# Second attention: the two normalisations of a step move from VectorE to ScalarE, with a bias made on GpSimd

## The reference, cut to what matters

```python
x = x + tanh(g_xattn[0]) * L0_xattn(layernorm(x), ctx, ctx)
x = x + tanh(g_ffn[0])   * L0_ffn(layernorm(x), ...)        # 64 experts, 8 per token, and a shared one
x = x + tanh(g_xattn[1]) * L1_xattn(layernorm(x), ctx, ctx, Wc, bc)
x = x + tanh(g_ffn[1])   * L1_ffn(layernorm(x), w_fc, w_proj)   # both products in emulated FP8

def L1_xattn(q, k, v, Wc, bc):      # 16 query heads of 16, 4 groups share a key and a value head
    scores = einsum('bghsd,bgtd->bghst', qh, kh) / sqrt(16)
    out = einsum('bghst,bgtd->bghsd', softmax(scores), vh)
    return out.reshape(b, s, 256) @ Wc.T + bc
```

## Time and profile before

| | |
|---|---|
| median of 3 runs | 1281.42 us (1279.56 to 1288.4) |
| the profiled execution's own time | 1274.8 us |
| its span | 1273.0 us |
| DVE busy over the span | 1050.5 us (83%) |
| PE / POOL / ACT busy | 883.2 / 718.4 / 702.0 us |
| second attention, steps 4 to 35 | from 883.4 to 1099.7 us of the span |

### The profile page before, as it was taken

One profiled execution on the slowest core, in us unless ns is written; L12 is line 12 of the kernel. 1 busy time (PEld: TensorE's weight loads), 2 busy tenths in 40 slices (PEclk: granted clock), 3 DMA queues, 4 the chain that ended last, 5 costly groups with the idle time before them and its releaser, 6 DMA issues.

```text
span 1273.0 us, 31296 instructions
## 1 busy us (share of the span) xinstructions
PE 883.2 (69%) x9384; PEld 626.0 (49%) x9394; DVE 1050.5 (83%) x2644; ACT 702.0 (55%) x1370; POOL 718.4 (56%) x800
## 2 busy tenths in 40 slices
PE   5789984465405888786777777756687778576665
PEld 3445552333204777675666666634455555322332
DVE  6789997988804889997589999966998888598998
ACT  4679994455303656655455555533555555515763
POOL 3557773777777565555347776456878882280000
PEclk9899995555557999999799999968899999888887
DMA  5977771222226999997899999985223330000011
GB/s 132 260 234 230 225 220 63 88 96 101 103 98 220 330 308 326 325 323 251 255 311 326 324 308 326 293 201 105 72 83 93 93 87 13 1 0 1 34 46 53
DMA packets 198114, 221.48 MB, mean 174 GB/s; under 512 B 44957, under 2 KB 176862, under 8 KB 197726
## 3 DMA queue, kind: packets, MB, share of 16 engines
q1 hardware_dynamic: 173406, 152.70, 39.0%
q0 software_dynamic: 24576, 67.14, 16.5%
HBM read 114.64 MB, written 105.12 MB: 173 GB/s over the span
## 4 chain that ended last, share of the span: by engine, by line
DMA 26%; DVE 23%; POOL 19%; issue 15%; PE 7%; ACT 5%; SPq 4%; DVEq 0%; POOLq 0%; ACTq 0%
DMA xs<-V 12%; POOL xs L757 7%; DMA V<-ys,idx 4%; DVE arena L1557 4%; POOL region L734 3%; DMA arena<-in_wpairs 3%; POOL arena L734 3%; DVE HM L1525 3%; DMA xs<-arena,V 2%; DMA arena<-ys,idx 2%; POOL V L734 2%; DVE x L1442 2%; DVE arena L1555 2%; ACT arena L804 2%; PE bank L1618 1%
## 5 line engine op out<-in xcount | busy, mean ns | idle before, releaser
L757 POOL DMA_INDIRECT xs<-V x192 | 191.1, 996 | 117.4 <-DMA xs<-V 59.8
L1734 PE MATMUL bank<-arena,region 128*128 128x128 f16 x2496 | 227.8, 230 | 0.4 <-ACT arena L919 0.3
L1808 PE MATMUL bank<-arena 128*128 128x128 f16 x1536 | 152.9, 224 | 96.5 <-DMA arena<-xs 95.9
L1734 PEld LDWEIGHTS bank<-arena,region 128*128 (+1 forms) x2496 | 174.3, 103 | 6.9 <-issue 0.8
L1808 PEld LDWEIGHTS bank<-arena 128*128 128x128 f16 x1536 | 102.8, 100 | 106.8 <-DMA arena<-xs 106.7
L919 ACT COPY arena<-bank 128x1024 f16<-128x1024 f16 x96 | 96.8, 1008 | 92.3 <-PE bank L1808 92.0
L934 ACT CAST arena<-arena 64x512 f16<-64x512 f32 x96 | 59.3, 618 | 140.0 <-DVE arena L1476 138.3
L804 ACT ACTIVATE arena<-bank 128x512 f32<-128x512 f32 x192 | 108.1, 604 | 47.8 <-PE bank L1618 47.4
L1066 DVE TENSOR_REDUCE arena<-bank 128x8 f32<-128x512 f32 x192 | 122.6, 679 | 10.6 <-PE bank L1604 8.8
L1460 DVE COPY arena<-bank 128x1024 f16<-128x1024 f16 x96 | 65.3, 681 | 78.8 <-PE bank L1808 78.0
L1837 PE MATMUL bank<-region,arena 128*128 x384 | 91.4, 278 | 51.4 <-DVE arena L1490 38.6
(11 more groups left out here) (229 smaller groups left out, 2253.0 us busy)
## 6 DMA issues: line engine op xcount, KB each, us to landing
arena<-xs SPq DMA_DIRECT2D x384, 128.0 KB
ys<-arena SPq DMA_DIRECT2D x96, 512.0 KB
xs<-idx SPq DMA_DIRECT2D x52, 256.0 KB, 3.1
arena<-in_wpairs SPq DMA_DIRECT2D x32, 256.0 KB, 2.9
arena<-in_wpairs SPq DMA_DIRECT2D x64, 128.0 KB, 3.2
out<-arena SPq DMA_DIRECT2D x16, 256.0 KB, 2.2
xs<-idx SPq DMA_DIRECT2D x8, 384.0 KB, 3.7
xs<-V POOLq DMA_INDIRECT x192
```

Of the source, the lines that this page charges most:

```text
L757: pool.indirect_dma_start(xs[half_of(t)], bass.IndirectOffsetOnAxis(ap=at_row[:, t, n % 8:n % 8 + 1], axis=0), ROW[t % NROW], None).then_i ...
L1734: mm = pe.matmul(o, lhs(a, w, k), rhs(a, w, k), start=(n == 0), stop=(n == 3 * KT - 1))
L1808: mm = pe.transpose(tpm[q // 2][:, q % 2, m, :], RAW[g % 2][:, q, m * P:(m + 1) * P], rcv("ident"))
```

## The change

VectorE's two normalisations of a step (`x - mean`, times `rs`) go. ScalarE makes them as `rs * x + away`, with `away = -mean * rs`; its instruction is an Identity activation whose scale and bias are columns of one element per partition. They stand in ScalarE's step behind the copy Q2 and ahead of the copy ONT: first the query of t+3, then `XD` of t-4. GpSimd makes `away` in `deviations`: one product of mean and -1, beside variance plus epsilon, and one of that and `rs`, behind the power. `deviations` now also waits for the normalised tiles whose `away` it overwrites. `rs2` is counted after the last product. VectorE's wait for `rs2` moves down, ahead of its statistics of t-3; the largest magnitude of `XD` stays where it was and waits for `LND["out"]`, which ScalarE counts now. ScalarE's second attention is written out whole in place of the loop.

```diff
+    away = sb("away", [P, 4, 1])
+    minus = sb("minus", [P, 1])
...
-                pool.wait_ge(ve2, n)
-                pool.tensor_tensor(rs[:, at, :], ve[:, at, :], neghalf[:, :].unsqueeze(1).to_broadcast([P, k, 1]), ALU.pow).then_inc(rs2, 1)
+                if inside(t + 2):
+                    pool.wait_ge(LNA["out"], STAT_BASE[2] + t + 3)
+                if inside(t - 5):
+                    pool.wait_ge(LND["out"], t - 4)
+                pool.tensor_tensor(away[:, at, :], mv[:, at, 0:1], minus[:, :].unsqueeze(1).to_broadcast([P, k, 1]), ALU.mult).then_inc(ve2, 1)
+                pool.wait_ge(ve2, 3 * n - 2)
+                pool.tensor_tensor(rs[:, at, :], ve[:, at, :], neghalf[:, :].unsqueeze(1).to_broadcast([P, k, 1]), ALU.pow).then_inc(ve2, 1)
+                pool.wait_ge(ve2, 3 * n)
+                pool.tensor_tensor(away[:, at, :], away[:, at, :], rs[:, at, :], ALU.mult).then_inc(rs2, 1)
...
+                def normed(dst, src, n, l):
+                    act.activation(dst, src, ACT.Identity, bias=away[:, n, :], scale=rs[:, n, :]).then_inc(l["out"], 1)
...
+                    if layer == 1 and t + 4 >= 1 and inside(t + 3):
+                        act.wait_ge(rs2, t + 4)
+                        normed(XG[(q + 3) % NXG].rearrange("p g (n w) -> p g n w", n=npair)[:, :, :, 0:2 * d].rearrange("p g n (k d) -> p g n k d", d=d),
+                               tile_x(t + 3).rearrange("p (n k g d) -> p g n k d", n=npair, g=G, d=d), 1 - j, LNA)
+                    if layer == 1 and inside(t - 4):
+                        act.wait_ge(rs2, t + 4)
+                        if past(t, 6):
+                            act.wait_ge(F["tp_ready"], t - 5)
+                            act.wait_ge(F["am_done"], t - 5)
+                        normed(XD[j], tile_x(t - 4), 2 + j, LND)
...
-                sweep(act, step, LAST[layer], 12 if layer else 4)
+                if layer == 0:
+                    sweep(act, step, LAST[layer])
+                else:
+                    for t in range(-3, LAST[layer] + 1):
+                        step(t, t % NKD)
...
-                    if t + 4 >= 1 and (inside(t + 3) or inside(t - 4)):
-                        dve.wait_ge(rs2, t + 4)
-                    if inside(t - 4):
-
-                        if past(t, 6):
-                            dve.wait_ge(F["tp_ready"], t - 5)
-                        norm(t - 4, 2 + j, 3, XD[j], tile_x(t - 4))
-                    if inside(t + 3):
-                        query(t + 3, 1 - j, (q + 3) % NXG)
                     if inside(t - 4):
                         dve.wait_ge(LND["out"], t - 3)
                         dve.tensor_reduce(AM[:, bass.ds(t - 4, 1)], XD[j], AX.X, ALU.max, apply_absolute_value=True).then_inc(F["am_done"], 1)
                     sums_within(t, 4)
+                    if t + 4 >= 1 and (inside(t + 3) or inside(t - 4)):
+                        dve.wait_ge(rs2, t + 4)
                     if inside(t - 3):
                         dve.wait_ge(a["x_done"], t - 2)
                         stats(t - 3, 3 - j, 3)
```

More of the change, by code:

```diff
@@ L632, in _ @@
             pool.memset(ZERO, 0.0).then_inc(half_set, 1)
-            pool.wait_ge(half_set, 3)
+            pool.memset(minus[:, :], -1.0).then_inc(half_set, 1)
+            pool.wait_ge(half_set, 4)
             def rstd(t, j, layer):
```

## The result

The changed kernel takes 1322.9 us (median of 4 runs, 1317.4 to 1327.36) against 1281.88 (4 runs, 1279.56 to 1288.4): ratio 1.0322, 95% interval 1.028 to 1.0364, so it is slower, by 41 us. The forecast was +34.1 us and 1315. The profiled execution took 1319.2 us with a span of 1317.4, 44.4 more than the span before.

What follows compares the result with a forecast made beforehand. DVE and POOL were taken as both close to full, with a new loop through ACT's normalisation to set the pace. Terms 0.7 + 9.5 + 19.8 + 4.1 = 34.1 us gave 1315 us, range 1298 to 1335.

Steps and rivals of the forecast that it cites:

- steps -3 to 3: Start of the second attention, without largest magnitude, pace set by loads and gathers: +0.7 us.
- The loop: Steps 9 to 27: largest magnitude waits for ACT's second normalisation, closing a one-step loop of 8.1 us; +19.8 us.
- Identity: ACT's new normalisation instruction, 128 x 256 float32 in SBUF: 0.59 us each, between 0.40 and 0.68.
- The rounding steps: Steps 4 to 8: the weights' rounding lies on the loop, 11.9 us for each of four steps; +9.5 us.
- Steps 28 to 35: Few or no sums, PE's order sets the pace: later ONT and a slower last chain, +4.1 us.
- PE's own round: PE's pass through its list in a main step: 5.5 us, 6.5 with ONT 1.0 us later, under the loop.
- POOL: Two added products a step: about 0.5 us, period 7.42 to 7.9 us, just under the loop's 8.1.
- rival 2: Steps 9 to 25: products held up by DVE's adds make POOL the bound, 8.8 us a step, 1327 us; chance 0.1.
- 1 (DVE relieved): Steps 3 to 27: DVE saves 0.73 us each, POOL's additions absorbed; -18 us, 1263 us; chance 0.04.
- 3: ACT delivers before DVE comes, only POOL's extra 0.5 us counts over 22 steps: +11 us, 1292 us; chance 0.1.
- 4 (low clock in the main steps): PE idles more and its clock stays low, 1.35 us in each of 19 steps: +26 us, 1341 us; chance 0.1.
- 5: Identity needs another table than Exp: 1.28 us loads in 28 steps, +36 us more, 1351 us; chance 0.02.

Runs made afterwards that it cites:

- e4: Changed kernel, but DVE again makes the normalisation its largest magnitude reads, ACT only the query's: ratio 1.0055 to the kernel before.
- e7: Changed kernel with ACT's copy ONT moved ahead of both normalisations: ratio 1.0256 to the kernel before.
- e8: Changed kernel with the largest magnitude at the end of DVE's step and ACT's order Q2, ONT, XD's normalisation, query's: ratio 1.0022 to the kernel before.
- e1: Changed kernel with DVE's largest magnitude moved to the end of its step, behind sums and statistics: ratio 1.0117 to the kernel before.
- e5: Changed kernel run again without edit, on a chip where the kernel before takes 1585 us: ratio 1.0196 to the kernel before.
- e2: Changed kernel without POOL's two products, ACT's bias being the epsilon column, so the mean isn't subtracted: ratio 1.0216 to the kernel before.
- e3: Kernel before with only POOL's two products added, their result read by no one: ratio 0.9967 to the kernel before.
- e6: Second run of the e1 kernel, largest magnitude at the end of DVE's step: ratio 1.0152 to the kernel before.
- e12: Third run of the e1 kernel, on a chip where the kernel before takes 1590 us: ratio 1.011 to the kernel before.

## Why the prediction was right

The sum's terms, in the profiled executions. The first stretch starts at DVE's last copy of the expert stage (L1483 before, L1503 after), the others at DVE's maxima:

| stretch | forecast | measured |
|---|---|---|
| steps -3 to 3 | +0.7 | -0.6 (46.85 to 46.25) |
| steps 4 to 8 | +9.5 | +11.3 (46.2 to 57.5) |
| steps 9 to 27 | +19.8 | +22.6 (135.5 to 158.05) |
| steps 28 to the last largest magnitude | +4.1 | +5.7 (34.1 to 39.85) |
| the attention | +34.1 | +39.0 |

The other 5.4 of the 44.4 us are 9.5 more ahead of the attention, in the unchanged first expert stage, where PE waits for gathered rows (105.7 us at L1828 after, 96 before), and 4.1 less behind it. They belong to this pair of executions; the medians differ by 41.0.

**The loop: right.** The step of 1016.35 against the forecast pieces: maxima to end of weighting 2.50 (forecast 2.50), to Q2's end 2.44 (2.44), to the largest magnitude 1.14 (1.04), and 2.04 from a largest magnitude to the next maxima (1014.31 to 1016.35; 2.02). That is 8.12, and 18 steps, from weighting 10 to weighting 28, average 8.2 (148.1 us) where I took 8.1. e4, e7 and e8 show it by intervention.

**Identity: 0.59 us forecast, 0.594 measured,** and 1.09 for the pair, which overlap by 0.10.

```profile
L817 ACT ACTIVATE arena<-x,away,rs 128x256 f32<-128x256 f32 x64 | 35.7, 594 | 4.2 <-POOL away L665 3.5
```

What I had wrong is that the first would begin 0.10 us ahead of Q2's end: in the main steps it begins 0.02 behind it (1021.29 to 1021.31), in e1 too, and behind ONT in e7. That 0.1 us a step is about 2 us of the 2.8 missing in the main steps.

**The rounding steps: mechanism right, size low.** Weighting to Q2's end in step 8 is 943.67 - 939.88 = 3.79 us, exactly the value of the slow step that I took. I had assumed about half of the four at the low clock; they took 11.24, 12.39, 13.39 and 12.09 us against 11.9 forecast each, and the granted clock of the stretch fell from 0.89 to 0.79.

**Steps 28 to 35: the sizes right, 1.6 us from elsewhere.** For ONT late I took 1.0 + 2.5 = 3.5 us from weighting 28 to 33; e5 takes 3.4 more than before there (29.8 for 26.4). After takes 4.9 more, and the 1.6 us between the two are one step, the last, of 6.8 us for 5.2: TensorE was at its low level in it (L1710's four matmuls at 1137.18 took 1.92 us for 1.03). The last chain, from weighting 33 on, took 0.7 more (0.6).

**PE's own round: too short.** For the main steps I gave it 6.5 us with ONT a microsecond late. The experiments with the largest magnitude moved show it as a loop of PE and ACT together, of 7.10 us against 6.3 to 6.4. I had added ONT's delay to PE's list, and not asked whether ACT's list comes back to PE: exponentials and Q2 follow ONT's consumer through the scores. This didn't harm the forecast, since 8.1 is longer. In e1 each step from 27 to 33 takes 0.5 to 1.8 us more than before, which its expectation left out.

**POOL: too dear.** The answer to the earlier trace rows, `deviations` in the same step as above:

```profile
1016.78 0.21 POOL L656 TENSOR_TENSOR ve<-mv,epsilon 128x2 f32<-128x2 f32 x1
1016.93 0.21 POOL L661 TENSOR_TENSOR away<-mv,minus 128x2 f32<-128x2 f32 x1
1017.07 0.73 POOL L663 TENSOR_TENSOR rs<-ve,neghalf 128x2 f32<-128x2 f32 x1
1017.88 0.20 POOL L665 TENSOR_TENSOR away<-away,rs 128x2 f32<-128x2 f32 x1
...
1018.24 1.15 POOL L744 DMA_INDIRECT region<-ys,idx  x1 [0.16 <-issue]
```

From the first to the gather is 1.46 us, against 1.25 in the earlier trace rows: +0.21, not +0.5, since neighbours overlap. A product that starts inside one of DVE's adds takes up to twice as long (0.44 us from 960.49, inside an add that ends at 960.87, 0.06 ahead of the product): the second one averages

```profile
L665 POOL TENSOR_TENSOR away<-away,rs 128x2 f32<-128x2 f32 x25 | 9.9, 397 | 2.0
```

so 0.2 us above its 0.20 when free. The Trainium skill (SBUF — State Buffer, the practical consequences of the shared port) states such a contention between DVE with two SBUF inputs and GpSimd; these rows agree. Its price was the rest of the add, 0.2 us in the mean and far below the whole add that rival 2 charged, and e2 and e3 show none in the time.

**The rivals.** 1 (DVE relieved): DVE is relieved by 12.2 us and the kernel slower, so busy share was the wrong guide. The Trainium skill (Perfetto Trace Analysis, Optimizing Scalar/DVE Operations) says that giving a saturated DVE's work to Scalar or GpSimd may make sense; here it did not, with 107.18 of 158.00 us busy where 119.39 of 135.50 had been. 2 and 3: e2, e3. 4 (low clock in the main steps): no on this chip, 0.99 granted; but in e1, e6, e7 and e12 it did fall there, to 0.87 to 0.89, so a chance of 0.1 was not too much. 5: one table load in the attention, as before, and none more for 64 Identities:

```profile
L814 ACT ACT_TABLE_LOAD x1 | 1.3, 1283 | 1.1 <-PE bank L1638 1.1
```

**Which of my signs held.** Idle of 1.5 to 2 us ahead of the largest magnitude in nearly every step: in all but two, though somewhat longer, 2.14 to 2.54 in steps 10 to 27, and 72.6 in all. PE's idle ahead of L1708 1 us longer: 1.48 for 0.39. POOL waits for means again: yes. Adds wait less for gathers than 12.7 us: 10.3, in two waits, both ahead of step 4 (874.30 and 884.69), so in the main steps they vanish as the sum had it. But 10.2 of the 12.7 us of before lie ahead of step 4 too (863.63 and 875.49): the prediction read all of them, and all 8.7 us of waits for `rs`, of which 3.4 lie outside too, as waits of the main steps. No term of the sum rests on it.

**How much was luck.** The forecast was low in three of its four terms, by 6.2 us together, and high in the first, by 1.3, so little was hidden by errors that cancel. The size of the total was tied to the chip: on one where the kernel before takes 1585 us the same loop cost 28 us, below the forecast's 34.

## What to carry to other kernels

An instruction moved to an idle engine takes that engine's place in time: ask what its new predecessor waits for, and whether its reader can run ahead of that. Here the reader's engine also fed the predecessor, and a saving of 0.73 us became a loop of 8.1 us; the sum of such a loop's pieces, taken from one step of the timeline, gave the period to 2%. And before closing a case with one loop, cut it: the second one (7.10 us, through ONT) had been invisible beneath it, and only both reorderings together (e8) gave the time back.

## What the runs showed of the hardware

- Neighbours on ACT overlap by about 0.10 us or not at all. In 27 of 32 steps of after the first Identity starts 0.02 or 0.03 us behind the end of the copy Q2 ahead of it; in the other five, an early one and steps 5 to 8 (943.56 for an end at 943.67 in step 8), it starts 0.10 to 0.11 ahead of it. A copy behind a copy (1264.71 before 1264.81 in e7) and ONT behind the Identities (1022.31 before 1022.40) overlap by about 0.10. So the operands alone don't decide it; what does was not tried.
- On the chips where the kernel before takes 1584 to 1590 us, counts of PE come 1.5 to 2.7 us behind the modelled ends of its matmuls in many steps, several within 0.2 us of one another (1286.01 to 1286.20 in e1), and ACT, or DVE in e3, stands still until then. The instruction that this hits differs between kernels (L868, L851, L835, L839). On the chips at about 1280 us the attention shows none.
- The same change cost 41 us on one chip and 28 on another. The loss of a loop is what it exceeds the former bound by, and that bound differed (122.1 us for 17 steps on one, 131.8 in e3 on the other).
- TensorE's granted clock in those 17 steps was 0.99 in after and 0.97 in e5 and e2, and 0.87 to 0.89 in e1, e6, e7 and e12. Ahead of the slow matmuls shown in e1 PE had idled for 4.18 us; its waits at the same place in after are 1.5 us at most.
- A product of 128 x 2 on POOL takes 0.20 us, and 0.41 to 0.47 us in 13 of 25 steps of after, when it starts inside one of DVE's adds.
